# A decoder layer on one core: transposes of the probabilities in row halves, and a new order of five steps around them

## The reference

```
# self attention, 16 heads of 64
Q, K, V = x W_Q + b_Q, x W_K + b_K, x W_V + b_V
attn = softmax(Q K^T / 8, over keys)          # (b, h, 128, 128)
x = layernorm(x + (attn V) W_O + b_O)         # "x1"
# second block: queries from x, keys and values from the context;
# attention over the HEADS of one position, 16 x 16 for each position
scores[b,s,h,g] = q[b,s,h] . k[b,s,g] / 8
attn = softmax(scores, over g);  out = attn v # "x2" after Wo, residual, norm
x = layernorm(x + out.transpose.reshape @ Wo^T + bo)
# feed forward: light branch and heavy branch for all 128 tokens of a batch
x = layernorm(x + gelu(rms(x) w1 + b1) w2 + b2  (light)  + the same (heavy))
```

## Time and profile before

| | |
|---|---|
| median of 3 runs | 410.6 us |
| the profiled execution, time | 410.04 us |
| its span in the profile | 408.2 us |
| granted TensorE clock | 0.998 of full |
| PE busy | 397.0 us, 97% |
| weight loads busy | 342.8 us, 84% |
| DVE busy | 286.8 us, 70% |
| ACT busy | 240.2 us, 59% |
| POOL busy | 147.7 us, 36% |

### The profile page before, as it was taken

One profiled execution on the slowest core, in us unless ns is written; L12 is line 12 of the kernel. 1 busy time (PEld: TensorE's weight loads), 2 busy tenths in 40 slices (PEclk: granted clock), 3 DMA queues, 4 the chain that ended last, 5 costly groups with the idle time before them and its releaser, 6 DMA issues.

```text
span 408.2 us, 15943 instructions
## 1 busy us (share of the span) xinstructions
PE 397.0 (97%) x6580; PEld 342.8 (84%) x6580; DVE 286.8 (70%) x661; ACT 240.2 (59%) x813; POOL 147.7 (36%) x224
## 2 busy tenths in 40 slices
PE   7999899999999999999999999999999999999995
PEld 6788788888888888788988888888988888888874
DVE  4593786965857787866849678677747878677545
ACT  4686654844756584745567465655567566547350
POOL 1540543431523354431413454323315445323223
PEclk9999999999999999999999999999999999999999
DMA  7900112210110213110110213100201110210001
GB/s 267 359 4 8 35 29 53 77 40 2 28 35 10 46 26 86 43 29 8 32 25 16 47 32 88 39 16 10 45 11 27 42 37 19 51 38 21 27 26 53
DMA packets 43646, 19.27 MB, mean 47 GB/s; under 512 B 36592, under 2 KB 40944, under 8 KB 43584
## 3 DMA queue, kind: packets, MB, share of 16 engines
q1 hardware_dynamic: 42592, 16.62, 15.8%
q0 software_dynamic: 560, 1.38, 0.9%
q10 hardware_dynamic: 432, 0.34, 0.3%
HBM read 8.88 MB, written 1.05 MB: 24 GB/s over the span
## 4 chain that ended last, share of the span: by engine, by line
PE 86%; DVE 5%; SPq 3%; DMA 2%; issue 2%; ACT 1%; POOL 0%; POOLq 0%; ACTq 0%; DVEq 0%
PE ps L1226 7%; PE ps L1171 7%; PE ps L1047 7%; PE ps L1075 7%; PE ps L1130 7%; PE ps L1151 7%; PE ps L1139 6%; PE ps L1027 5%; PE ps L1029 4%; PE ps L1028 4%; PE ps L1181 4%; PE ps L1066 4%; PE ps L1106 3%; SPq L314 3%; PE ps L1165 2%; PE ps L1159 2%
## 5 line engine op out<-in xcount | busy, mean ns | idle before, releaser
L541 ACT ACTIVATE p<-ps,neg_max 128x128 f32<-128x128 f32 x256 | 90.3, 385 | 40.7 <-DVE neg_max L810 40.7
L411 POOL TENSOR_TENSOR p<-p,row_inv 128x1024 f32<-128x1024 f32 x32 | 60.7, 1898 | 61.9 <-DVE row_inv L816 61.9
L534 ACT ACTIVATE pt<-ps 128x512 f32<-128x512 f32 x62 | 34.4, 626 | 47.9 <-PE ps L1130 47.9
L541 ACT ACTIVATION_READ_ACCUMULATOR p<-ps,neg_max 128x1 f32 x256 | 57.8, 226 | 0.0
L810 DVE TENSOR_REDUCE neg_max<-ps 128x4 f32<-128x512 f32 x64 | 41.5, 672 | 4.8 <-PE ps L1226 4.0
L756 DVE TENSOR_TENSOR ot<-ps,bv 128x512 f32<-128x512 f32 x32 | 22.0, 688 | 29.7 <-PE ps L1151 29.5
L1130 PE MATMUL ps<-ident,p 128*128 128x128 f32 x256 | 34.7, 279 | 1.7 <-issue 0.9
L1226 PE MATMUL ps<-kt,qt 64*64 64x128 f32 x1024 | 35.2, 275 | 0.0
L1139 PE MATMUL ps<-x1t,wq 128*64 128x64 f32 x1024 | 33.5, 224 | 0.9 <-DVE v2s L766 0.9
L1139 PEld LDWEIGHTS ps<-x1t,wq 128*64 128x64 f32 x1024 | 31.3, 138 | 2.2 <-issue 1.1
L1171 PE MATMUL ps<-wo,ot 128*128 128x128 f32 x256 | 32.7, 281 | 0.5 <-DVE ot L756 0.5
(11 more groups left out here) (159 smaller groups left out, 837.1 us busy)
## 6 DMA issues: line engine op xcount, KB each, us to landing
v<-v2s SPq DMA_DIRECT2D x256, 32.0 KB
xg<-x_t SPq DMA_DIRECT2D x4, 256.0 KB, 3.6
cg<-ctx_t SPq DMA_DIRECT2D x4, 256.0 KB, 3.7
wo<-w_o SPq DMA_DIRECT2D x2, 512.0 KB, 9.2
xres<-x_nat SPq DMA_DIRECT2D x15, 64.0 KB, 1.7
pt<-w_qk SPq DMA_DIRECT2D x3, 256.0 KB, 5.2
out<-x2b SPq DMA_DIRECT2D x3, 256.0 KB, 2.3
x2b<-w_v SPq DMA_DIRECT2D x1, 512.0 KB, 6.3
```

What stands on the lines that cost most here:

```text
L411: nc.gpsimd.tensor_tensor(ph, ph, row_inv[:, 8 * half:8 * half + 8].unsqueeze(2).to_broadcast([T, 8, T]), ALU.mult).then_inc(p_ready, 1)
L534: nc.scalar.activation(pt[:, u * BANK:(u + 1) * BANK], bank(T_BANK[u]), ACT.Copy).then_inc(pt_ready, 1)
L541: last = nc.scalar.activation(p[:, hd * T:(hd + 1) * T], bank(S_BANK[q])[:, pos * T:(pos + 1) * T], ACT.Exp, bias=neg_max[:, hd:hd + 1], a ...
```

## The change

Five edits, in the diff below.

1. `transpose_p` takes a whole half (eight heads) and transposes each head in two pieces: the rows (queries) 0 to 63 and 64 to 127 of p, each with its 64x64 part of the identity. The pieces of the upper rows go to one PSUM bank and those of the lower rows to another, so that each of the four banks now holds 64 queries of eight heads. ACT's four copies put them back with a strided destination (`pt_part`), so pt has the same content as before.
2. On POOL, the bias sum on x1, which waits for x1, comes behind the first multiplication of p instead of ahead of it: the multiplication stands right behind the root.
3. x1 is written by `scalar_tensor_tensor`, with the mean as a scalar and the reciprocal root as a broadcast second tensor, instead of by `tensor_scalar` with two scalars.
4. On DVE, the reciprocal of the first eight row sums comes between the two `block_diagonal` instructions instead of behind x1.
5. On DVE, `regrouped` comes ahead of both halves of `q2_out` instead of between them.

```diff
+        def pt_part(u):
+            half, e = u // 2, u % 2
+            return (pt[:, half * 8 * T:(half + 1) * 8 * T].rearrange("p (h e q) -> p e h q", h=8, e=2)[:, e],
+                    bank(T_BANK[u]).rearrange("p (h q) -> p h q", h=8))
...
@@ POOL: rstd1 ends behind the root, its last part becomes x1_biased
+            def x1_biased(s, b_par):
                 if isinstance(s, int) and s == 1:
                     pool.wait_ge(in_bo2, 16)
                 pool.wait_ge(x1_ready, s)
...
                 if bc:
                     rstd1(s, b_par)
-                for half in range(2):
-                    if a:
-                        pool.wait_ge(inv_ready, 2 * s + half + 1)
...
+                if a:
+                    over_sum(s, 0)
+                if bc:
+                    x1_biased(s, b_par)
+                if a:
+                    over_sum(s, 1)
@@ ACT
-                    nc.scalar.activation(pt[:, u * BANK:(u + 1) * BANK], bank(T_BANK[u]), ACT.Copy).then_inc(pt_ready, 1)
+                    dst, src = pt_part(u)
+                    nc.scalar.activation(dst, src, ACT.Copy).then_inc(pt_ready, 1)
@@ DVE
-                nc.vector.tensor_scalar(x1[:], t1[:], mv1[:, 0:1], rs1[:, 0:1], ALU.subtract, ALU.mult).then_inc(x1_ready, 1)
+                nc.vector.scalar_tensor_tensor(out=x1[:], in0=t1[:], scalar=mv1[:, 0:1], in1=rs1[:, 0:1].to_broadcast([T, D]),
+                                               op0=ALU.subtract, op1=ALU.mult).then_inc(x1_ready, 1)
...
                     block_diagonal(s, 0)
+                if a and bc:
+                    inverse_sums(0)
+                if d:
                     block_diagonal(s, 1)
                 if bc:
                     x1_out(s)
...
                 if a:
-                    inverse_sums(0)
                     score_max(2)
...
-                    q2_out(s, 0)
                 if d:
                     regrouped(s)
                 if bc:
+                    q2_out(s, 0)
                     q2_out(s, 1)
@@ PE
-            def transpose_p(n, u):
-                if u % 2 == 0:
-                    pe.wait_ge(p_ready, 2 * n + u // 2 + 1)
-                for i in range(4):
-                    hd = 4 * u + i
-                    last = nc.tensor.transpose(bank(T_BANK[u])[:, i * T:(i + 1) * T], p[:, hd * T:(hd + 1) * T], ident[:])
-                last.then_inc(mm_t, 1)
+            def transpose_p(n, half):
+                pe.wait_ge(p_ready, 2 * n + half + 1)
+                for i in range(8):
+                    hd = 8 * half + i
+                    for e in range(2):
+                        rows = slice(HALF * e, HALF * e + HALF)
+                        mm = nc.tensor.transpose(bank(T_BANK[2 * half + e])[:, i * HALF:(i + 1) * HALF],
+                                                 p[rows, hd * T:(hd + 1) * T], ident[rows, rows])
+                        if i == 7:
+                            mm.then_inc(mm_t, 1)
```

More of the change, by code:

```diff
@@ L392, in rms2, with over_sum @@
                 nc.gpsimd.tensor_tensor(x2b[:, bass.ds((s - 2) * D, D)], x2[:], bdl_row[:], ALU.add).then_inc(x2b_ready, 1)
+            def over_sum(s, half):
+                pool.wait_ge(inv_ready, 2 * s + half + 1)
+                ph = p[:, half * 8 * T:(half + 1) * 8 * T].rearrange("q (h k) -> q h k", h=8)
+                nc.gpsimd.tensor_tensor(ph, ph, row_inv[:, 8 * half:8 * half + 8].unsqueeze(2).to_broadcast([T, 8, T]),
+                                        ALU.mult).then_inc(p_ready, 1)
             def step(s, h, g, phase, a, bc, d):
@@ L405, in step @@
                     rstd1(s, b_par)
-                for half in range(2):
-                    if a:
-                        pool.wait_ge(inv_ready, 2 * s + half + 1)
-                        ph = p[:, half * 8 * T:(half + 1) * 8 * T].rearrange("q (h k) -> q h k", h=8)
-                        nc.gpsimd.tensor_tensor(ph, ph, row_inv[:, 8 * half:8 * half + 8].unsqueeze(2).to_broadcast([T, 8, T]),
-                                                ALU.mult).then_inc(p_ready, 1)
+                if a:
[4 more added lines that the diff above has]
+                    over_sum(s, 1)
                 if d:
@@ L427, in _ @@
             rstd1(B, 1)
+            x1_biased(B, 1)
             minus_max2(LAST)
@@ L1244, in step @@
                 if bc:
-                    transpose_p(s - 1, 2)
-                    transpose_p(s - 1, 3)
+                    transpose_p(s - 1, 1)
                 if phase == 0 and a and bc:
@@ L1347, in step @@
                     transpose_p(s, 0)
-                    transpose_p(s, 1)
                 if phase == 3 and not static:
@@ L1380, in _ @@
                 step(s, s // 2, s // GB, s % GB, s < B, 1 <= s <= B, s >= 2)
-            transpose_p(B - 1, 2)
-            transpose_p(B - 1, 3)
+            transpose_p(B - 1, 1)
             pe.wait_ge(wup_split, 2)
```

## The result

The changed kernel took **429.24 us** (median of 4 runs, 426.83 to 431.24) against 410.38 for the kernel before: a ratio of 1.046, 95% interval 1.040 to 1.051. That is slower, as forecast, by the mechanism forecast, and 5.0 us later than the predicted 424.2, just outside the range (its upper end was 428; one of the four runs lies inside it). The profiled execution took 429.38 us with a span of 427.6 (forecast 422.1), at TensorE's full granted clock as before.

What follows compares the result with a forecast made beforehand. TensorE, busy 97% of 408.2 us, was taken as the bound. Held x1 less row-half savings, +12.5 in the loop plus the steps outside, gave +13.9: span 422.1, time 424.2 us; range 402.5 to 428.

Steps and rivals of the forecast that it cites:

- price of a row half: PE's sixteen row-half transposes of half of p: 0.48 us instead of 0.85, a saving of 0.37 per half.
- a held x1: DVE's x1 waits for POOL's first-half multiplication to end, so PE's x1 transpose comes 1.61 us later per step.
- phase 3's wait for q2: Regrouping first delays q2's first half in phase 3; PE's projections lose the first-half saving and 0.20 us more, three times.
- first halves: Row-half transposes of p's first half on PE: 0.37 us saved per step in phases 0 to 2, none in phase 3.
- second halves: Row-half transposes of p's second half on PE: 0.37 us saved in phases 0 and 1, 0.32 in 2 and 3.
- ahead of the loop: Steps 0 to 2: -0.75 and -0.1 us in steps 0 and 1, +1.1 in step 2.
- behind it: Step 15 and the end: +1.3 us in step 15, at most 0.1 saved at the end.
- Rival A: Three-operand x1 runs beside POOL, not held, and row halves work: 0.33 us late start, 406.6 us in all; chance 0.40.
- regrouping first: DVE's regrouped output ahead of q2's halves: cost 0 outside phase 3, ready 3.7 us behind the x1 transpose, O2 wanting 4.08.
- The start: Steps 0 and 1: two halves before the first x1 save 0.75 us.
- ACT's copies: ScalarE's copies of pt, same count, shorter runs: cost 0, hidden by PE's value products; at worst doubled, scores waiting tenths.
- Rival D: POOL becomes the bound in the second half; 0.1 us every step would add 1.5 to any case; no stall expected.

Runs made afterwards that it cites:

- the best version: The kernel before with the transposes in row halves and regrouping first in phases 0, 1 and 2 only, without the three other edits: 406.34 us.
- no_rows: The changed kernel with the old 128x128 transposes, all other edits kept: 430.09 us, ratio 1.047 to the kernel before.

## Where the prediction was right, and the steps that failed

The direction and its cause came as forecast; the size failed in two steps. The larger one is a term that was put at nothing: twice the transposes were taken to cost their own length and nothing else, and PE stood still for 3.4 us more in the loop. The smaller one is the price of a row half. Either alone would have left the time inside the range. The table goes by the prediction's own steps; all from the profiled executions, span +19.4 where +13.9 was forecast.

| term | forecast | measured |
|---|---|---|
| a held x1, per step | +1.61 | +1.56 |
| phase 3's wait for q2, per group | +0.20 | +0.18 |
| first halves, 9 steps | -3.3 | -3.2 |
| second halves, 12 steps | -4.1 | -2.6 |
| hitches in the loop | 0 | +3.4 |
| the loop, 12 steps | +12.5 | +16.8 |
| ahead of the loop | +0.25 | +1.3 |
| behind it | +1.2 | +1.2 |

- **x1 held**: right, and right in size. Its value is what is left when the other measured terms are taken from the loop (18.8 / 12); phase 2 of the changed kernel against the best version gives the same without hitches: 18.93 - 0.34 - 17.02 = 1.57. Over 14 steps it is 22 us, more than the whole 19.4. Since a wait took up the 0.4 us of before, the hitches may be counted as 3.8 instead of 3.4; x1 is then 1.53. Rival A, at 0.40, spoke of the three-operand form as unknown; what decided was the inputs, as the earlier trace rows said for x2. Rival A's price of 0.33 for x1's late start, by the early reciprocal, measured 0.24.
- **The price of a row half** failed in size. I took 0.48 us from the q2 products' 31 ns a piece; it is 0.64, 40 ns a piece, inside the outer bounds of 0.25 and 1.71 but 0.16 off where the range allowed 0.1. A second half brings 0.2, not 0.37. The first halves came out right by chance: 0.18 from the pieces, and 0.18 from regrouping first, which I had priced at nothing ("Cost 0"). In the trace of before O2 already waited that long for the regrouped output, within the 1.03 us from 151.09 to 152.12 of the earlier trace rows, with no idle time printed beside it.
- **The hitches** are the step that failed most. They stood in no term and no rival: the sum took 256 more loads and 256 more products for free beyond their own length. They are the largest part of the 5.5 us excess: 3.4. That they hang on the place in PE's instructions is shown; that PE lacks instructions there is inferred.
- **The start**: no gain of 0.75. The transposes there take 1.21 instead of 1.94 us, but PE then waits 0.64 us for ACT's copies of pt: the clause "hidden by the value products" had no value products ahead of it in step 0. The rest is PE's first transposes, which start 0.47 us later (30.69 against 30.22; 30.38 in no_rows); why, no run settles.
- **ACT's copies**: no longer than before, 611 ns each against 626; only in step 0 does PE wait for them.
- Rival D did not come: POOL's second half is followed by no wait of PE in the loop.

In the table a second half's value is from the changed kernel against no_rows, step by step (0.88 a group), and a first half's from 2.98 - 2.62. The excess of 5.5 us in span is then 3.4 (hitches) + 1.5 (second halves) + 1.1 (start), less 0.55 (x1's size over 12 steps).

## What to carry to other kernels

When two engines are to be overlapped, look at which inputs of the shorter instruction lie in SBUF, not at the operation; a held instruction shows no idle time, only a duration that ends just behind the neighbour's. If the overlap is wanted, one input from PSUM, or a neighbour cut in two, gives much of it back: here 18.6 and 12.4 of the 18.9 us that the changed kernel lost. Neither was faster than the kernel before; the fastest versions are those in which the two don't meet. An edit that adds instructions to an engine at 97% needs a second look at runs of its shortest products, even if its busy time falls.

## What was not expected of the hardware

- PE's instructions come in 54 transfers of 16 KB; with 13,672 loads and products that is some 250 in each. Where one lands during a run of 31 to 40 ns products PE can stand for 0.2 to 0.9 us. Where it falls depends on how many instructions stand ahead: 36 fewer, with no change to the work, moved the best version from 406.34 to 405.26 us. That PE lacks its next instructions there is inferred from landing and restart; the trace has no record of it. What makes a transfer start late is open.
- Row pieces of 64x64 in turn: 40 ns each; by row group, and so by bank: 59 ns (0.94 / 16); whole 128x128: 106 ns.
- A DVE instruction that reads PSUM and a broadcast column took 0.34 us inside a 1.90 us POOL instruction, where the same from SBUF took 1.65.
